# Two-layer block on one core: order and step numbers of the first layer's vector, scalar and store work

## The chip, the cores and the metric

The kernel runs on one core of a Trainium2 chip. The metric is device time in microseconds, the median of several runs. The engines are named as the profile names them: PE (TensorE, with PEld for its weight loads), DVE (VectorE), ACT (ScalarE), POOL (GpSimd) and SP (SyncE, which here only issues DMAs). Each works through its own instructions in the order in which the program lists them, and they meet at semaphores.

## What is computed

Two layers, each `x + attention(norm(x)) * silu(ffn(norm(x)))`, over 4 sequences of 512 tokens with 512 features. The change lies in the first layer and in the first work of the second.

```python
# layer 0: softmax attention, 32 query heads of 16 over 8 key/value heads, no mask
q, k, v = xn @ Wq, xn @ Wk, xn @ Wv
attn = softmax((q @ k.T) * 16 ** -0.5).astype(float16)
s = (attn @ v) @ Wo
# layer 0: FFN between Walsh-Hadamard transforms (fwht)
h = fwht(xn * SU_ug) / 64
h = silu(h @ W_gate.T * (Wscale_gate * 64)) * (h @ W_up.T * (Wscale_up * 64))
h = fwht(h * SU_dp) / 64
g = silu(h @ W_down.T * (Wscale_dp * 64))
x = x + s * g
# layer 1: gated delta-rule recurrence (6 heads of 64) and an FFN with sign(up), sign(down) weights
x = x + recurrent(layernorm(x)) * silu(ffn_sign(layernorm(x)))
```

## The kernel before

The kernel is one program in two parts, `layer0` and `layer1`. `layer1` is not touched, apart from what the end of `layer0` prepares for it.

**The loop.** Layer 0 runs a loop over steps `t` that every engine walks in its own block of code, `for t in range(TEND)`. `b = t // 64` is the batch (sequence) and `m = t % 64` the step in it; there are 256 steps of four batches and 39 steps behind them (`b == B`, called batch 4 here), in which the last batch is finished and layer 1 begun. A step number such as `OUT_STEP` or `K_STEP` says at which `m` a piece of work is listed. Step numbers stand in tuples at the top of the file (lines 37 to 57).

**Attention.** A score group is one block of 128 queries of one key/value head with its 4 query heads: four matmuls of 128x512 into four PSUM banks. It is listed at every odd step. PE's `scores` (L1134) waits until the four exponentials of the group before have read the banks (`p_ready`). DVE then takes four row maxima (`row_max`, L638), each followed by ACT's `exps` (L944), which writes the probabilities. The time from one group's scores to the next is called a pair below, because it spans two steps. `turn_probs` (L352) on SP transposes the probabilities by DMA at even steps, and PE's `weigh` (L1150) multiplies them with the values for two groups at a time, at every fourth step. DVE transposes tokens (L676, L700), and PE's projection by `wo` is L1122.

**What is laid around it.** In steps `m < 32` PE does the down projection of the batch before, 6 matmuls a step (L1179). In steps `m >= 32` it does the gate and up projections, 8 matmuls a step (L1165), gate chunks at even steps and up chunks at odd ones. A chunk goes through ACT `tanh_gate` (L956), DVE `gate_mul` (L644) and `up_mul` (L657), then ACT `high_rows` (L913, a 16-bit copy of the product in `th`) and POOL `low_rows` (L454, the remainder). `up_mul` writes the buffer that `low_rows` of the chunk before has read. In an odd step `m > 32` the order on DVE is row maximum 0, `gate_mul`, row maxima 1 to 3, `up_mul`. On ACT it is `tanh_gate`, exponential 0, `high_rows`, exponentials 1 to 3.

**Keys and queries.** `project_k` (L1102) is listed at `K_STEP` 57 on PE, and ACT's `evict_k` (L920) at 58. It copies the keys of the next batch to the buffer `kst`, and waits until all heads of the present batch have been loaded from `kst` and `qst` (DMAs of SP: `load_k` L310 at `m % 8 == 6`, `load_q` L320 at `m % 8 == 2`). The last of these, a `load_q`, is listed on SP at step 58.

**The end of a block of tokens.** For each of the four blocks of 128 tokens of the batch before: DVE `scale_down` (L711) at `DOWN_END` 8, 16, 24, 32; ACT `tanh_down` (L964) one step later; DVE `second_gate` (L716) one more step later, which is listed ahead of the row maxima of that step. At `OUT_STEP` the attention output is projected (PE L1122), at +1 comes `gated` (L722) on DVE and POOL's add (L459), at +3 the store of `x1` from the buffer `th` (SP L388). There are two `th` buffers, so `tanh_down` of block 2 waits for the store of block 0, and the first `up_mul` of the next batch, which uses the same memory, for the store of block 2.

**Batch 0** has extra work: the FFN weights are transformed and split into 16-bit halves. PE transforms (L1075, L1076) and transposes the normed rows of later batches (L1054); ACT `evict_x` (L876) copies these transposes out, at the steps `TURN_STEP`; POOL adds pairs of weights (L413, L414, L423, L424, L448).

**Batch 4** has 8 steps of attention left (`ATT = 8` is the distance between a step and the exponentials listed at it). At `m == 3` DVE lists the first work of layer 1: `next_stats` (L766, L769), `weight_max` (L727, twice) and `next_scale`, at 9 `next_split` (L783, L786), at 12 `weight_low` (L751), at 13 `column_scales`; ACT `weight_high` (L969) at 9. SP loads the raw weights at `RAW_AT` (L344), ACT takes their signs at `SIGN_AT` (L975). PE transposes the split rows at `NEXT_STEP` (L1200), ACT evicts them at `EVICT_STEP` (L979), and `project_next` (L1211) ends the layer.

## Time and profile before

| | us |
|---|---|
| median of 3 runs | 1400.39 (1399.33 to 1401.78) |
| the profiled execution | 1401.55 |
| its span (first to last instruction) | 1399.8 |
| PE busy | 1259.5 (90%) |
| DVE busy | 1050.2 (75%) |
| ACT busy | 787.6 (56%) |
| POOL busy | 524.7 (37%) |
| layer 0, up to the first layer-1 operation | 768.8 |

How it is read: busy time is the sum of the operations of an engine. In the timeline a row is one operation, or a run of equal ones ("x4"), with its start and length; the bracket is the time that the engine stood idle before it and what ended that idle time. "PEclk" is the clock that TensorE was granted in each slice, in tenths of full speed. Layer 1 takes the last 631 us, in four like stretches.

### The profile page before, as it was taken

Reading aid. Unit: us, or ns where it says so; the run is one execution under the profiler, and the core shown is the slowest. Engines: PE = TensorE matmul, PEld = TensorE weight load, DVE = VectorE, ACT = ScalarE, POOL = GpSimd, SP = SyncE. Lnnn points to the kernel's source line nnn. Section 1 sums busy time; section 2 is a strip of 40 time slices with the busy share of each in tenths; the row PEclk is TensorE's granted clock in tenths of the full one; section 3 lists DMA queues with packets and bytes.
Section 4 is the critical chain, followed back from the end, with each engine's and each line's share of the span. In section 5 each row is a group of like instructions: output and inputs, shape, how many; then the busy total and the mean of one; then the engine's idle time right before and its main releaser. Section 6 shows DMA issues by size and latency. Waiting matters only on the chain. (4 is left out here: it accounts for less than half of the span.)

```text
span 1399.8 us, 23475 instructions
## 1 busy us (share of the span) xinstructions
PE 1259.5 (90%) x8738; PEld 643.5 (46%) x8738; DVE 1050.2 (75%) x1823; ACT 787.6 (56%) x1306; POOL 524.7 (37%) x434
## 2 busy tenths in 40 slices
PE   5777977988798897889959999999999999999998
PEld 2332333333333333333324545865477555855475
DVE  6678875778677786778883986868956976968845
ACT  4775765667676685667836752355433652355431
POOL 3589852012211221012301573328431573328431
PEclk9999999999999999999989999999999999999999
DMA  6655643676567765786777024010131024001121
GB/s 238 199 138 95 110 84 72 108 155 136 104 112 156 141 118 96 137 158 119 127 208 283 22 58 90 10 38 27 44 81 38 9 58 91 17 31 40 42 40 46
DMA packets 346561, 135.59 MB, mean 97 GB/s; under 512 B 312176, under 2 KB 333392, under 8 KB 343888
## 3 DMA queue, kind: packets, MB, share of 16 engines
q1 hardware_dynamic: 334032, 132.52, 42.4%
q10 hardware_dynamic: 12416, 1.57, 1.0%
q8 instruction: 70, 1.15, 0.4%
q14 instruction: 43, 0.35, 0.1%
HBM read 44.87 MB, written 17.87 MB: 45 GB/s over the span
## 5 line engine op out<-in xcount | busy, mean ns | idle before, releaser
L1165 PE MATMUL bank<-rows,both 128*128 128x512 f16 x1024 | 250.2, 391 | 38.8 <-DVE th L657 22.4
L944 ACT ACTIVATE probs<-vpair,top_n 128x512 f16<-128x512 f32 x256 | 170.5, 687 | 141.3 <-DVE top_n L638 141.2
L638 DVE TENSOR_REDUCE top_n<-vpair 128x1 f32<-128x512 f32 x256 | 169.3, 682 | 64.5 <-PE bank L1134 64.0
L1179 PE MATMUL bank<-dn,h 128*128 128x512 f16 x768 | 182.6, 386 | 0.0
L1165 PEld LDWEIGHTS bank<-rows,both 128*128 128x128 f16 x1024 | 95.9, 100 | 176.5 <-DVE th L657 36.6
L944 ACT ACTIVATE probs<-bank,top_n 128x512 f16<-128x512 f32 x256 | 164.4, 687 | 0.0
L638 DVE TENSOR_REDUCE top_n<-bank 128x1 f32<-128x512 f32 x256 | 163.3, 678 | 0.0
L454 POOL TENSOR_TENSOR h<-th,h 128x512 f16<-128x512 f32 x61 | 70.5, 1155 | 225.0 <-ACT h L913 225.0
L2246 PE MATMUL bank<-rows,both 128*128 128x512 f16 x512 | 117.3, 380 | 0.0
L1179 PEld LDWEIGHTS bank<-dn,h 128*128 128x128 f16 x768 | 71.3, 99 | 93.7 <-issue 17.8
L2262 PE MATMUL bank<-both,hid 128*128 128x512 f16 x512 | 111.2, 379 | 0.0
L2230 PE MATMUL bank<-rows,both 128*128 128x512 f16 (+1 forms) x456 | 104.0, 379 | 0.9 <-PEq L160 0.9
L1134 PE MATMUL vpair<-qk 32*128 32x512 f16 x256 | 50.5, 390 | 35.4 <-ACT probs L944 35.4
L2262 PEld LDWEIGHTS bank<-both,hid 128*128 128x128 f16 x512 | 50.1, 98 | 60.4
L2246 PEld LDWEIGHTS bank<-rows,both 128*128 128x128 f16 x512 | 48.1, 99 | 55.0
L2230 PEld LDWEIGHTS bank<-rows,both 128*128 128x128 f16 (+1 forms) x456 | 43.6, 98 | 55.6 <-issue 4.4
L1621 POOL TENSOR_TENSOR big<-big,both 128x384 f32<-128x384 f32 x32 | 32.0, 1025 | 94.5 <-DMA big<-t_scratch 70.2
L657 DVE SCALAR_TENSOR_TENSOR th<-bank,hsc,tg 128x512 f32<-128x512 f32 x64 | 48.0, 751 | 22.1 <-POOL h L454 10.8
L467 POOL TENSOR_TENSOR otok<-oblk,rl 128x256 f16<-128x256 f32 x25 | 15.5, 619 | 125.0 <-DVE rl L684 125.0
L956 ACT ACTIVATE tg<-bank,usc 128x512 f32<-128x512 f32 x64 | 44.0, 687 | 32.5 <-DVE th L657 21.6
L1575 POOL TENSOR_TENSOR hid<-sil 128x512 f32<-128x512 f32 x24 | 33.1, 1379 | 62.4 <-DVE sil L1695 62.4
L1134 PEld LDWEIGHTS vpair<-qk 32*128 32x128 f16 x256 | 12.5, 91 | 91.8 <-ACT probs L944 54.3
(357 smaller groups left out, 2556.5 us busy)
## 6 DMA issues: line engine op xcount, KB each, us to landing
h<-in_ug SPq DMA_DIRECT2D x8, 1024.0 KB, 6.5
lt_scratch<-big SPq DMA_DIRECT2D x16, 384.0 KB, 2.8
dn<-in_down SPq DMA_DIRECT2D x2, 2048.0 KB, 11.5
x_scratch<-th SPq DMA_DIRECT2D x16, 256.0 KB, 3.1
res<-x_scratch SPq DMA_DIRECT2D x16, 256.0 KB, 4.3
out_x<-res SPq DMA_DIRECT2D x16, 256.0 KB, 2.0
both<-in_w SPq DMA_DIRECT2D x2, 1548.0 KB, 11.4
t_scratch<-tok SPq DMA_DIRECT2D x16, 192.0 KB, 2.1
```

Source lines behind the costliest of these rows:

```text
L454: pool.tensor_tensor(h16(ft, 1), row32, h16(ft, 0), ALU.subtract).then_inc(S["row_lo"], 1)
L638: v.tensor_reduce(top_n[:, i:i + 1], SC_[n % G][:, :], AX.X, ALU.max, negate=True).then_inc(S["max_done"], 1)
L657: v.scalar_tensor_tensor(row32, GB[n % 2][:, :], hsc[:, ft:ft + 1], tg[:, :], ALU.mult, ALU.mult).then_inc(S["gb_took"], 1)
L944: a.activation(probs[:, k % TAKEN, j * T:(j + 1) * T], SC_[j][:, :], ACT.Exp, bias=top_n[:, i:i + 1]).then_inc(S["p_ready"], 1)
L956: a.activation(tg[:, :], GB[n % 2][:, :], ACT.Tanh, scale=gsc[:, ft:ft + 1]).then_inc(S["tanh_ready"], 1)
L1134: pe.matmul(SC_[j][:, :], qs[32 * j:32 * j + 32, u % SLOTS, qt * P:(qt + 1) * P], ks[32 * j:32 * j + 32, u % SLOTS, :], start=True, stop=T ...
L1165: mm = pe.matmul(GB[n % 2][:, :], w[:, kt, col:col + P], xnb(b, kt), start=r == 0, stop=r == 2 * KT - 1)
L1179: mm = pe.matmul(bk, h16(ft, r // 2)[:, rows], dn16(ft, r % 2), start=j == 0 and r == 0, stop=j == FT - 1 and r == 2)
L1575: pool.tensor_tensor(sqf[m % 2], sil[:, ORDER[m], :], sil[:, ORDER[m], :], ALU.mult).then_inc(S["sq_r"], 1)
L2230: mm = pe.matmul(bk, lhs(i, kt), rhs(j, kt), start=n == 0, stop=n == 3 * KT - 1)
L2246: mm = pe.matmul(fbank[ht % 2][:, :], up[:, kt, ht * P:(ht + 1) * P], x_half(i, kt), start=kt == 0 and i == 0, stop=kt == KT - 1 and i == 1)
L2262: mm = pe.matmul(fbank[tt % 2][:, :], hid[:, i, ht, tt * P:(tt + 1) * P], down[:, ht, :], start=ht == 0 and i == 0, stop=ht == HT - 1 and ...
```

## The change

It moves work and adds or removes none, apart from one empty step at the end of the loop.

- `K_STEP` 57 becomes 61: `project_k` on PE and `evict_k` on ACT are listed four steps later.
- `OUT_STEP` and `OUT_LAST` (20, 22, 28, 35) become (20, 22, 26, 34): blocks 2 and 3 are projected, gated and stored earlier. `TEND` becomes 294.
- ACT: `tanh_down` becomes the first of its step instead of one of the last; `high_rows` stands ahead of exponential 0 instead of behind it; `evict_x` stands ahead of the exponentials instead of behind them.
- The first work of layer 1 is listed later: the DVE block from step 3 to step 8, `next_split` 9 to 11, `weight_low` 12 to 14, `column_scales` 13 to 15, ACT `weight_high` 9 to 11, the exponential of `negA` 10 to 12; the transposes and their evictions 19 and 20 to 21 and 22; the first three raw loads 11, 12, 13 to 13, 14, 15; two of the signs 22, 23 to 23, 24.

```diff
-OUT_STEP = (20, 22, 28, 35)
-OUT_LAST = (20, 22, 28, 35)
-NEXT_STEP, EVICT_STEP = 19, 20
+OUT_STEP = (20, 22, 26, 34)
+OUT_LAST = (20, 22, 26, 34)
+NEXT_STEP, EVICT_STEP = 21, 22
 XRES_STEP = (17, 19, 24, 25)
-Q_STEP, V_STEP, K_STEP = 5, 43, 57
+Q_STEP, V_STEP, K_STEP = 5, 43, 61
...
-RAW_AT = (11, 12, 13, 21, 23, 24, 25, 26)
-SIGN_AT = (18, 19, 20, 21, 22, 23, 26, 34)
+RAW_AT = (13, 14, 15, 21, 23, 24, 25, 26)
+SIGN_AT = (18, 19, 20, 21, 23, 24, 26, 34)
...
-                if b == B and m == 3:
+                if b == B and m == ATT:
                     next_stats()
                     weight_max(0)
                     next_scale()
...
-                if b == B and m == 9:
+                if b == B and m == ATT + 3:
                     next_split()
                     weight_scales()
-                if b == B and m == 12:
+                if b == B and m == ATT + 6:
                     for kt in range(KT):
                         weight_low(kt)
-                if b == B and m == 13:
+                if b == B and m == ATT + 7:
                     column_scales()
...
+                if b and m - 1 in DOWN_END:
+                    tanh_down((b - 1) * TT + DOWN_END.index(m - 1))
                 if b < B and m > FFN_STEP and m % 2:
                     tanh_gate(b, (m - FFN_STEP) // 2)
-                if paired:
-                    exps(G * (ta // 2))
                 if 0 <= fb < B and fm > FFN_STEP and t % 2:
                     high_rows(fb, (fm - FFN_STEP) // 2)
-                if paired:
-                    for j in range(1, G):
-                        exps(G * (ta // 2) + j)
                 if t in TURN_STEP:
                     evict_x(KT + TURN_STEP.index(t))
+                if paired:
+                    for j in range(G):
+                        exps(G * (ta // 2) + j)
...
-                if b and m - 1 in DOWN_END:
-                    tanh_down((b - 1) * TT + DOWN_END.index(m - 1))
-                if b == B and m == 9:
+                if b == B and m == ATT + 3:
                     weight_high()
-                if b == B and m == 10:
+                if b == B and m == ATT + 4:
```

## Rows read from the trace of the kernel before

**Rows 1.** Page, section 2: POOL busy and TensorE clock, 40 slices of 35 us

```profile
POOL 3589852012211221012301573328431573328431
PEclk9999999999999999999989999999999999999999
```

**Rows 2.** Waits: engine, line, releaser; total us, times, longest us

```profile
ACT kst L920 <- DMA qk<-qst: 19.8, 3, 7.5
DVE th L716 <- ACT th L964: 19.8, 11, 7.8
PE bank L1054 <- ACT rows L876: 13.1, 5, 3.6
DVE th L657 <- POOL h L454: 10.8, 47, 0.6
```

**Rows 3.** Timeline, 328 to 334 us, batch 1: start, length, engine, line, operation [idle]

```profile
328.75 0.39 PE L1134 MATMUL vpair<-qk 32*128 32x512 f16 x2
...
329.17 0.69 DVE L638 TENSOR_REDUCE top_n<-vpair 128x1 f32<-128x512 f32 x1 [0.41 <-PE bank L1134]
...
332.48 0.75 DVE L657 SCALAR_TENSOR_TENSOR th<-bank,hsc,tg 128x512 f32<-128x512 f32 x1 [0.23 <-POOL h L454]
...
333.61 0.39 PE L1134 MATMUL vpair<-qk 32*128 32x512 f16 x2
```

**Rows 4.** Timeline, 214 and 376 to 389 us, around evict_k, batches 0, 1

```profile
214.69 0.60 ACT L920 ACTIVATE kst<-bank 128x512 f16<-128x512 f32 x1 [5.61 <-DMA qk<-qst]
...
376.75 0.39 PE L1134 MATMUL vpair<-qk 32*128 32x512 f16 x2
...
379.57 2.44 SPq L320 DMA_DIRECT2D qk<-qst  x4
383.34 0.60 ACT L920 ACTIVATE kst<-bank 128x512 f16<-128x512 f32 x1 [7.45 <-DMA qk<-qst]
...
388.93 0.39 PE L1134 MATMUL vpair<-qk 32*128 32x512 f16 x2
```

**Rows 5.** Timeline, 264 to 300 us, around tanh_down, batch 1

```profile
264.06 0.39 PE L1134 MATMUL vpair<-qk 32*128 32x512 f16 x2 [0.24 <-ACT probs L944]
...
265.16 1.28 DVE L638 TENSOR_REDUCE top_n<-vpair 128x1 f32<-128x512 f32 x2
...
294.95 0.58 SPq L388 DMA_DIRECT2D x_scratch<-th  x1
...
295.48 1.29 ACT L944 ACTIVATE probs<-vpair,top_n 128x512 f16<-128x512 f32 x2 [1.28 <-DVE top_n L638]
...
298.01 0.39 PE L1134 MATMUL vpair<-qk 32*128 32x512 f16 x2 [0.24 <-ACT probs L944]
...
298.30 0.63 ACT L964 ACTIVATE th<-fd 128x512 f32<-128x512 f32 x1 [0.34 <-DMA x_scratch<-th]
...
299.57 1.28 DVE L638 TENSOR_REDUCE top_n<-vpair 128x1 f32<-128x512 f32 x2
```

**Rows 6.** Timeline, 313 to 318 us, steps 33 to 35 of batch 1

```profile
313.98 1.21 SPq L388 DMA_DIRECT2D x_scratch<-th  x1
...
317.38 0.75 DVE L657 SCALAR_TENSOR_TENSOR th<-bank,hsc,tg 128x512 f32<-128x512 f32 x1 [3.34 <-DMA x_scratch<-th]
```

**Rows 7.** Timeline, 60 to 62 us, batch 0: an evict_x and its waiter

```profile
60.62 0.59 ACT L876 ACTIVATE rows<-bank 128x512 f16<-128x512 f16 x1
...
61.26 0.38 PE L1065 MATMUL bank<-amax,allone 128*128 128x1 f32 x2 [2.06 <-ACT rows L876]
```

**Rows 8.** Timeline, 720 to 763 us, end of layer 0

```profile
720.70 0.61 PE L1134 MATMUL vpair<-qk 32*128 32x512 f16 x2 [13.20 <-ACT probs L944]
...
721.64 5.14 PE L1179 MATMUL bank<-dn,h 128*128 128x512 f16 x12
...
741.81 0.70 DVE L700 STREAM_TRANSPOSE oT<-otok 128x512 f16<-128x512 f16 x1
...
762.84 5.45 PE L1211 MATMUL bank<-rows,both 128*12 128x512 f16 x24
```

## The prediction, made before the changed kernel was run

> **What bounds the kernel now.** I read the page first, then the table of waits, then the timeline of each place that the diff touches. The page says that TensorE was granted nearly its full clock, but for one slice at 700 to 735 us [rows 1]. PE is 90% busy over the span, so what can be won is its idle time and its slow stretches in layer 0. Layer 1, 631 us, has no edit. Within layer 0 the pace is not set by PE alone: two groups share a cycle scores, row maxima, exponentials, next scores, and whatever is queued between these on DVE or ACT lengthens a pair. The waits table names the places that the diff aims at: `evict_k` behind a DMA, 19.8 us in 3 waits; `second_gate` behind `tanh_down`, 19.8 in 11; PE behind an `evict_x`, 13.1 in 5; `up_mul` behind POOL's `low_rows`, 10.8 in 47 [rows 2]. A wait in that table is idle time of an engine and not yet time of the kernel, so each is priced below from the spacing of the scores.
>
> **Keys at step 61.** In batch 1 the copy of the keys waits for the last `load_q`, issued at 379.57, and ACT stands 7.45 us with the exponentials queued behind it; the pair takes 388.93 - 376.75 = 12.18 us [rows 4]. An ordinary pair of the same shape takes 333.61 - 328.75 = 4.86 [rows 3]. The gain is 12.18 - 4.86 = 7.3. Is the wait gone or only moved? The next scores would now come at 376.75 + 4.86 = 381.6, and the copy at step 62 stands behind those of that pair, 4 us or so later, at about 385.7 on the clock of now; the load had landed by 383.3. Gone, by 2 us. Batch 2 is taken by the table: 19.8 in three waits, less 7.45 and less 5.61 of batch 0 [rows 2, 4], leaves 6.7, and I count 6.7. In batch 0 steps 57 to 63 also carry down-weight transposes through the same single bank (`DN_AT`), so the projection at 61 should lengthen that pair; between no gain and 5.6 I take 2.7. The moved projection itself (4 matmuls) leaves one PE-filled pair and fills another: nothing. Past `load_k` on SP at step 62, which waits for `evict_k`: `load_k` is for heads needed several pairs later, and SP is idle at that time in batch 1 (it issues nothing between the `load_q` and the copy that it waits for). I price it at nothing; if SP had no slack it would cost the load's 2.5 us. **Sum: 7.3 + 6.7 + 2.7 = 16.7.**
>
> **high_rows ahead of exponential 0.** In the gate/up stretch `up_mul` waits 0.23 for POOL's `low_rows`, which waits for `high_rows`, behind exponential 0 [rows 3]. The row maximum that exponential 0 needs starts at 329.17 and ends at 329.86 [rows 3], and ACT, which comes out of `tanh_gate` at about 329.55, has 0.3 us free there, so the 0.62 us copy delays exponential 0 by at most 0.3 and exponential 1 not at all. Low end: the wait alone, 10.8 us in 47 [rows 2], counted only in the pairs that PE or `up_mul` bounds, about 6 of 16 in a batch: 6 x 0.23 = 1.4. High end: the whole copy, 0.62, in those six, 3.7. I take 2.5 a batch, 2.9 in batch 3 (no projections that fill PE), 1.1 in batch 0, where POOL is full: **9.0**, range 3 to 13.
>
> **tanh_down ahead of the exponentials.** At a step such as 264.06 the row maximum comes 265.16 - 264.06 = 1.10 after the scores, against 329.17 - 328.75 = 0.42 where nothing stands in front [rows 5, 3]. `second_gate` is late because the tanh came behind four exponentials. Ahead of them it is done before: 0.68 gained at blocks 0 and 1. But moving it also makes ACT do it before the exponentials of its own step, and for block 2 it waits for the store of block 0: issued at 294.95, the tanh starts at 298.30 after a wait on that DMA, while the exponentials of the same step start at 295.48 now [rows 5]. **This is a new wait.** Behind it are queued the four exponentials, and behind these PE's next scores and DVE's next maxima. The tanh still starts at 298.30, exponential 0 at 298.93, and the next scores 298.01 - 295.48 = 2.53 later, at 301.46: 3.45 later than now. The pair behind has its row maximum at 0.42 and not at 299.57 - 298.01 = 1.56, which gives back 1.14. So from there the batch runs 2.3 us late against now, and the 1.36 of blocks 0 and 1 are swallowed by the wait, unless the store comes earlier. SP works back to back in this stretch, so I take it that it doesn't. **Cost 2.3 in each of batches 1, 2 and 3.** In batch 4 block 2 has no exponentials behind it (8 steps only): nothing.
>
> **OUT_STEP 28 to 26, 35 to 34.** The first `up_mul` of the next batch waits 3.34 us for the store of block 2, issued at 313.98 [rows 6], with row maxima queued behind it. Two steps earlier (a pair, 3.7 us) the store lands before `up_mul` comes: 3.34 gained in three batches, 10.0. The four `wo` matmuls are only moved within steps where PE waits. At the start of a batch `high_rows` between exponentials 0 and 1 leaves too (about 0.45, the last pair of the gate/up stretch) in batches 2 to 4: 1.3. **Together with the cost above: 10.0 + 1.3 - 6.9 = 4.4.**
>
> **evict_x in batch 0.** PE waits for transposed rows that ACT copies behind four exponentials, as at 61.26 after a copy at 60.62 [rows 7]; 13.1 in 5 waits [rows 2]. Ahead of the exponentials the copy comes some 2.5 us earlier, but the exponentials each 0.6 later. From below 1, from above most of the 13.1 less six copies of 0.6, or 9.5. But POOL bounds part of this stretch, eight and nine tenths busy in the slices from 70 to 140 us [rows 1], and where it does an earlier copy gives nothing. I take **5**.
>
> **The end of layer 0.** Now the block of layer 1 holds the row maxima and PE stands 13.20 us before the scores at 720.70 [rows 8]. I looked for what it would leave if moved: the same DVE work still stands before `next_split` and `weight_low`, and the tokens' last transpose (741.81) and so the last output projections wait for it; `project_next` starts at 762.84 behind them [rows 8]. By the new order the transposed tokens come at about 742 again. PE gains 13 us early and waits them out later. I take **0**, from 6 worse to 2 better on this path, and the case that the bubble is really gained is a rival.
>
> Beside this a rule of the Trainium skill, in sentences the sum does without. Rows first: after the 13.20 us idle, 12 down matmuls took 5.14 us, 0.43 each, and 24 matmuls at 762.84 took 5.45, 0.227 each [rows 8]: the half clock of 1.2 GHz against 2.4. "TensorE: Matmul & The Clock Gate", section "HAM oscillation — how this bites in real kernels", says that a burst after an idle stretch starts cold and that the penalty is half of the throttled time; the trace agrees. It speaks against this change in one respect: the new hold at step 25 makes a fresh idle of PE of some 4 us per batch, which by it could add about 1 to 3 us each; it speaks for it at `evict_k`, where the idle goes.
>
> **Sum.** 16.7 + 9.0 + 4.4 + 5 + 0 = 35.1. From the profiled execution, 1401.55 - 35.1 = 1366.4; the median lies 1.16 below it, so 1365.3. I say **1365**.
>
> **The rivals.**
> 1. *The gains are smaller.* `high_rows` and `evict_x` pay at their low ends (3 and 1), and the hold at step 25 costs 4 in each batch rather than 2.3, as clock is lost with it: 16.7 + 3 + (11.3 - 12) + 1 - 2 at the end = 18, time 1382. For it: six of the terms are a choice between far ends. Chance 0.22.
> 2. *The end of the layer is won.* If what fixed the end was PE's work and not DVE's chain, the 13.20 us come free: 1352. For it: the largest single idle of PE. Against it: DVE's work is the same and ends at the same time. Chance 0.12.
> 3. *The key wait stays.* The change would not do what it says if the copy at step 62 still waited: for `load_q` of the next steps, or if SP is so late that its landing follows. Then 16.7 goes: 1382. Against it: the load had landed at 383.3. Chance 0.05.
> 4. *Slower.* The hold at step 25 feeds itself: with the copy of keys gone, SP's queue loses its pause of some 7 us per batch and comes later to the stores, each later store holding the exponentials one for one. It decides from about 12 us of extra lateness in each of three batches: 1365 + 36 = 1401 and beyond, say 1404. Against it: SP has idle time between batches. Chance 0.04.
>
> **How the numbers follow.** The forecast has 0.57, with its own range 1357 to 1374. The range 1352 to 1384 takes in rivals 1, 2 and 3 and leaves out their tails and rival 4. A difference of 0.2% (2.8 us) is about what a measurement of this kernel can tell from none. Faster: all cases but rival 4 and a thin edge, 0.93; same 0.03; slower 0.04.
>
> **What would show it.** Right: no `kst <- DMA` wait, the pair at steps 59 to 61 near 4.9; a wait `ACT L964 <- DMA x_scratch` of about 3 us in front of the exponentials of step 25, batches 1 to 3; no wait of `up_mul` on `x_scratch`; `second_gate` without a wait at steps 10 and 18; the first operation of layer 1 at 768.8 less 35, with PE idle behind step 8 of batch 4 instead of at step 5. Wrong: layer 1 longer or shorter than 631, a wait of SP on `evict_k` that reaches the scores, or a layer-0 tail that starts 13 us sooner behind the same batch 4.

## The result and the profile after

The changed kernel takes 1367.84 us (median of 4 runs, 1366.1 to 1369.64) against 1401.09 for the kernel before beside it: 0.9758 of its time, 95% interval 0.9728 to 0.9787. The forecast was 1365, from 1352 to 1384. The profiled execution has a span of 1367.5 us, 32.3 less than before; the sum had said 35.1. The first matmul of layer 1 starts at 738.34 (769.17 before), so 30.8 of the 32.3 lie in layer 0; the other 1.4 are in layer 1 (629.2 us long, 630.6 before), which no edit touches.

The page first: instruction counts and busy times are those of before within 6 us, so the whole difference is idle time and clock.

```profile
PE 1256.4 (92%) x8738; PEld 644.2 (47%) x8738; DVE 1045.0 (76%) x1823; ACT 785.3 (57%) x1306; POOL 525.1 (38%) x434
```

The waits that answer [rows 2] (total us, times, longest us):

```profile
DVE th L716 <- ACT th L964: 16.9, 6, 6.3
ACT th L964 <- DMA x_scratch<-th: 16.3, 3, 5.9
...
ACT probs L944 <- DMA probsT<-probs: 10.7, 1, 10.7
...
PE bank L1052 <- ACT rows L876: 5.8, 4, 2.8
...
DVE th L657 <- POOL h L454: 1.7, 1, 1.7
```

No wait of `evict_k` on a DMA is left (19.8 us before), nor the wait of the first `up_mul` on the store. `low_rows` holds `up_mul` once and not 47 times; PE's wait behind `evict_x` has fallen from 13.1 to 5.8, and `second_gate` no longer waits at steps 10 and 18. And there is a wait of 16.3 us, `tanh_down` of block 2 on the store of block 0, three times, longest 5.9. In the kernel before, the same table has it so:

```profile
ACT th L964 <- DMA x_scratch<-th: 1.4, 3, 0.8
```

Lines after 1030 are two lower than before (L1132 is `scores`, L1052 the transpose of rows, L1163 the gate/up matmul).

Around the keys, batch 1 (timeline: start, length, engine, line, operation; compare [rows 4]):

```profile
366.92 0.39 PE L1132 MATMUL vpair<-qk 32*128 32x512 f16 x2
...
370.24 2.44 SPq L320 DMA_DIRECT2D qk<-qst  x4
...
371.45 0.39 PE L1132 MATMUL vpair<-qk 32*128 32x512 f16 x2
...
375.58 0.59 ACT L920 ACTIVATE kst<-bank 128x512 f16<-128x512 f32 x1
```

The pair that took 12.18 takes 371.45 - 366.92 = 4.53, and the copy at 375.58 waits for nothing.

Around step 25, batch 1 (compare [rows 5]):

```profile
286.67 0.39 PE L1132 MATMUL vpair<-qk 32*128 32x512 f16 x2 [0.47 <-ACT probs L944]
...
287.66 1.50 SPq L388 DMA_DIRECT2D x_scratch<-th  x1
...
291.30 0.63 ACT L964 ACTIVATE th<-fd 128x512 f32<-128x512 f32 x1 [4.77 <-DMA x_scratch<-th]
...
291.83 1.25 ACT L944 ACTIVATE probs<-vpair,top_n 128x512 f16<-128x512 f32 x2
...
294.29 0.61 PE L1132 MATMUL vpair<-qk 32*128 32x512 f16 x2 [3.33 <-ACT probs L944]
...
294.84 4.36 PE L1177 MATMUL bank<-dn,h 128*128 128x512 f16 x13
...
299.13 0.39 PE L1132 MATMUL vpair<-qk 32*128 32x512 f16 x2
```

This is the new wait: the exponentials stand behind the tanh and the tanh behind a store. The pair takes 294.29 - 286.67 = 7.62 us where 3.67 is its length without a hold. The 13 matmuls behind it took 4.36 us, 0.335 each against 0.227 at full clock [rows 8], and PE has no gap from 294.29 to the next scores at 299.13: this next pair, 4.84 us, is as long as PE's slow matmuls make it.

The end of layer 0 (compare [rows 8]):

```profile
687.45 1.26 ACT L944 ACTIVATE probs<-vpair,top_n 128x512 f16<-128x512 f32 x2 [10.69 <-DMA probsT<-probs]
...
689.95 1.05 PE L1148 MATMUL bank<-probsT,vaug 128*32 128x256 f16 x16 [9.82 <-issue]
690.93 6.66 PE L1177 MATMUL bank<-dn,h 128*128 128x512 f16 x24
...
710.01 0.70 DVE L700 STREAM_TRANSPOSE oT<-otok 128x512 f16<-128x512 f16 x1
...
710.86 1.86 PE L1120 MATMUL bank<-wo,oT 128*128 128x512 f16 x4 [2.46 <-DVE oT L700]
...
732.02 5.45 PE L1209 MATMUL bank<-rows,both 128*12 128x512 f16 x24
```

PE's 13.20 us before the scores of step 7 are gone. In their place stand 9.82 before `weigh` and 2.46 before the first projection, with slow matmuls behind both. The last transpose is still what it waits for.

What ends the first of the two is on SP. The exponentials at 687.45 waited 10.69 us for a transpose of the probabilities, and SP issued it at 681.06, behind 15 loads for layer 1 that stand there from 667.51 on:

```profile
667.51 1.16 SPq L326 DMA_DIRECT2D rows<-x_scratch  x1
...
680.53 0.43 SPq L334 DMA_DIRECT2D both<-in_out_scale  x1
681.06 11.74 SPq L352 DMA_TRANSPOSE probsT<-probs  x4
```

The kernel before had the same loads at the same place; there the wait of the same exponentials is put down to the row maxima:

```profile
711.26 0.43 SPq L334 DMA_DIRECT2D both<-in_out_scale  x1
711.80 14.57 SPq L352 DMA_TRANSPOSE probsT<-probs  x4
...
718.17 1.28 ACT L944 ACTIVATE probs<-vpair,top_n 128x512 f16<-128x512 f32 x2 [14.14 <-DVE top_n L638]
```

Counted from the scores of step 5, that transpose landed after 14.0 us before and after 14.2 us now, and these exponentials started after 14.1 and 14.3. Two waits ended there within 0.2 us, one on DVE and one on SP's loads. The change moved the one that showed.

For the whole of layer 0, pair lengths worked out from the starts of the scores:

| pair | before | after |
|---|---|---|
| steps 59 to 61, batches 1, 2 | 12.18, 11.80 | 4.54, 4.54 |
| 25 to 27, batches 1, 2, 3 | 3.67, 3.67, 3.67 | 7.62, 8.48, 8.75 |
| 27 to 29, batches 1, 2, 3 | 4.81, 4.70, 5.29 | 4.84, 4.78, 4.62 |
| 33 to 37 (two pairs), batches 1, 2, 3 | 13.14, 13.20, 13.21 | 9.62, 9.62, 9.62 |
| the pairs from 39, 47, 51, 55 (and 43 in batch 3), batches 1 to 3 | 4.85 to 5.50 | 4.54 |
| step 5 of batch 4 to the first layer-1 matmul | 65.1 | 65.2 |

### The profile page after: what moved, and what is told of

Read it like the earlier page. It is cut to its first block and busy times, and to the rows that moved or that the text cites. A ratio compares the mean times of both kernels' runs of the same rounds, so it can differ in the third digit from the quotient of the medians.

```text
span 1367.5 us, 23475 instructions
## 1 busy us (share of the span) xinstructions
PE 1256.4 (92%) x8738; PEld 644.2 (47%) x8738; DVE 1045.0 (76%) x1823; ACT 785.3 (57%) x1306; POOL 525.1 (38%) x434
## 2 busy tenths in 40 slices
DMA packets 346561, 135.59 MB, mean 99 GB/s; under 512 B 312176, under 2 KB 333392, under 8 KB 343888
## 5 line engine op out<-in xcount | busy, mean ns | idle before, releaser
L1163 PE MATMUL bank<-rows,both 128*128 128x512 f16 x1024 | 244.9, 385 | 13.5 <-DVE th L657 9.7
L1163 PEld LDWEIGHTS bank<-rows,both 128*128 128x128 f16 x1024 | 95.6, 99 | 148.1 <-issue 21.6
L2244 PE MATMUL bank<-rows,both 128*128 128x512 f16 x512 | 118.8, 383 | 0.0
L1132 PE MATMUL vpair<-qk 32*128 32x512 f16 x256 | 50.8, 392 | 26.6 <-ACT probs L944 26.5
L459 POOL TENSOR_TENSOR th<-fd,xres 128x512 f32<-128x512 f32 x16 | 18.5, 1156 | 96.6 <-DVE fd L722 96.6
L1633 POOL TENSOR_TENSOR os_<-os_,both 128x6 f32<-128x6 f32 x16 | 23.3, 1459 | 80.6 <-DVE os_ L1991 80.6
L1686 DVE SCALAR_TENSOR_TENSOR rows<-pre,both,rows 128x512 f32<-128x512 f32 x36 | 40.8, 1133 | 17.1 <-ACT rows L2067 16.2
## 6 DMA issues: line engine op xcount, KB each, us to landing
both<-in_w SPq DMA_DIRECT2D x2, 1548.0 KB, 11.3
```

The costliest lines, as they stand in the source:

```text
L1132: pe.matmul(SC_[j][:, :], qs[32 * j:32 * j + 32, u % SLOTS, qt * P:(qt + 1) * P], ks[32 * j:32 * j + 32, u % SLOTS, :], start=True, stop=T ...
L1163: mm = pe.matmul(GB[n % 2][:, :], w[:, kt, col:col + P], xnb(b, kt), start=r == 0, stop=r == 2 * KT - 1)
L1686: v.scalar_tensor_tensor(c[:, :], src[:, i:i + T], cw[:, cm, i:i + 1], c[:, :], ALU.mult, ALU.add).then_inc(S["conv"], 1)
L2244: mm = pe.matmul(fbank[ht % 2][:, :], up[:, kt, ht * P:(ht + 1) * P], x_half(i, kt), start=kt == 0 and i == 0, stop=kt == KT - 1 and i == 1)
```

## The experiments

Each was timed beside the kernel before; the ratio is to that. The medians of the kernel before were 1400.0 (experiments 1 to 4), 1400.1 (5 to 7 and 10), 1403.1 (8, 9, 11) and 1403.0 us (12), and 1401.1 for the changed kernel above. "More" and "less than the changed kernel" are differences of medians from these different sessions. By the ratios the same differences are 19.6 us for experiment 1, 7.0 for 2, 13.7 for 3, 8.0 for 4, 6.7 for 6 and 7.4 for 7, each good to some 5 us; the intervals of 2, 4, 6 and 7 only just clear that of the changed kernel. Lengths of pairs are from one profiled execution each.

**1. The keys back at step 57.**

```diff
-Q_STEP, V_STEP, K_STEP = 5, 43, 61
+Q_STEP, V_STEP, K_STEP = 5, 43, 57
```

> The changed kernel with K_STEP put back to 57, nothing else. My sum: the wait of evict_k on the last load_q comes back in batches 1 and 2, pairs of 12.2 and 11.8 us in place of 4.5, less 0.8 for the projection that moves back: +7.3 and +6.9; in batch 0 a stall of some 5.5 again but without the pairs of 7.5 and 10.1 behind it, +2.7. Theory (the key wait was the largest term): about 1367.8 + 16.5 = 1384, range 1381 to 1387. Rival (the pairs around step 59 are set by PE or by high_rows, and the wait would only be taken over): below 1373.

Measured 1386.12 us, ratio 0.9898 (0.9881 to 0.9914): 18.3 more than the changed kernel. The wait is back as it was:

```profile
ACT kst L920 <- DMA qk<-qst: 19.7, 3, 7.3
```

The pairs at 59 took 12.2 and 11.9 us in batches 1 and 2, and in batch 0 the three pairs from 57 to 63 took 28.3 us against 25.5 in the changed kernel: 2.8. The key wait is the largest term, and nothing took it over.

**2. evict_x behind the exponentials again.**

```diff
-                if t in TURN_STEP:
-                    evict_x(KT + TURN_STEP.index(t))
                 if paired:
                     for j in range(G):
                         exps(G * (ta // 2) + j)
+                if t in TURN_STEP:
+                    evict_x(KT + TURN_STEP.index(t))
```

> The changed kernel with evict_x behind the exponentials again. It is only in batch 0 that anything can differ. The changed kernel reaches step 33 of batch 0 5.95 us sooner than the kernel before. Theory (this comes from evict_x, the only edit of that stretch but for tanh and high_rows, which have nothing to do there): +5 to +7, about 1373.5, and the scores of step 33 back near 135.4 us. Rival (POOL's weight pairs bound the stretch, so that the early lead of 9 us at step 21 is not evict_x's to keep): +0 to +2.

Measured 1373.92 us, ratio 0.9808 (0.9790 to 0.9827): 6.1 more. The scores of step 33 of batch 0 came at 136.2 us (129.5 in the changed kernel). At step 21 the changed kernel led this one by 11.3 us and at step 33 by 6.7. Of both, 1.5 stood already at the very first scores (48.1 and 49.6 us; in kernels with the changed kernel's start these came at 46.7 to 49.2), which leaves 9.8 and 5.2. So 4.6 of it was lost between steps 21 and 33, where POOL adds its weight pairs, but not the rest.

```profile
PE bank L1052 <- ACT rows L876: 13.2, 6, 3.6
```

**3. high_rows between exponentials 0 and 1 again.**

```diff
-                if 0 <= fb < B and fm > FFN_STEP and t % 2:
-                    high_rows(fb, (fm - FFN_STEP) // 2)
...
+                if paired:
+                    exps(G * (ta // 2))
+                if 0 <= fb < B and fm > FFN_STEP and t % 2:
+                    high_rows(fb, (fm - FFN_STEP) // 2)
                 if paired:
-                    for j in range(G):
+                    for j in range(1, G):
                         exps(G * (ta // 2) + j)
```

> The changed kernel with high_rows between exponentials 0 and 1 again. Theory: the pairs that the changed kernel has at 4.54 us go back to 4.85 (five or six per batch), the first two pairs of a batch from 4.37 and 3.67 to 4.65 and 4.13: 6 x 0.31 + 0.7 = 2.6 in each of batches 1 to 3, about 1 in batch 0 and 0.7 in batch 4: +9, about 1377, range 1374 to 1379. Rival (PE bounds these pairs, the gain came from other edits): +0 to +3, and no change of the 4.54 pairs.

Measured 1378.72 us, ratio 0.9856 (0.9839 to 0.9873): 10.9 more. The pairs of 4.54 us went back to 4.86 and 5.14, and:

```profile
DVE th L657 <- POOL h L454: 12.5, 48, 1.7
```

Ending a wait of 0.23 us in each pair, far down in the table, was worth some 9 to 11 us of the kernel.

**4. tanh_down of block 2 behind the exponentials, the others first.**

```diff
-                if b and m - 1 in DOWN_END:
+                if b and m - 1 in DOWN_END and m - 1 != DOWN_END[2]:
                     tanh_down((b - 1) * TT + DOWN_END.index(m - 1))
...
+                if b and m - 1 == DOWN_END[2]:
+                    tanh_down((b - 1) * TT + 2)
```

> The changed kernel, but tanh_down of block 2 alone goes back behind the exponentials; those of blocks 0, 1 and 3 stay first. In the changed kernel the pair of step 25 takes 7.62, 8.48 and 8.75 us in batches 1, 2 and 3 where 3.67 is its length without a hold, and the pair behind it 4.84, 4.78 and 4.62. Theory (the hold on the store of block 0 costs wall time one for one): the three pairs fall to 3.67 and the pairs behind them stay at 4.7 to 5.3: 4.0 + 4.8 + 5.1 = 13.9 less, at most 1.5 of it lost to row maxima behind a late second_gate, so about 1355, range 1353 to 1358. Rival (the hold is bubble that the next store or the first up_mul of the batch takes back, since the store of block 2 is listed only some pairs later): gain under 4, 1364 or above, with a wait of up_mul on the store.

Measured 1356.93 us, ratio 0.9701 (0.9680 to 0.9723): 10.9 less than the changed kernel, 3 us short of the arithmetic of the pairs and inside the range. The wait on the store has fallen from 16.3 to:

```profile
ACT th L964 <- DMA x_scratch<-th: 2.3, 3, 1.4
```

The pair at 25 took 4.22, not 3.67, in each batch. By the ratio the gain is 8.0 and not 10.9; the profiled execution of the changed kernel has dearer holds than most (see below). The edit also moves the tanh of block 2 in batch 4, and there it cost 1.4 (66.6 us from the scores of step 5 to layer 1, for 65.2). So the hold that the prediction named is real and is the change's largest loss.

**5. The kernel before with tanh_down first in its step, and nothing else of the change.**

```diff
+                if b and m - 1 in DOWN_END:
+                    tanh_down((b - 1) * TT + DOWN_END.index(m - 1))
                 if b < B and m > FFN_STEP and m % 2:
                     tanh_gate(b, (m - FFN_STEP) // 2)
...
-                if b and m - 1 in DOWN_END:
-                    tanh_down((b - 1) * TT + DOWN_END.index(m - 1))
```

> The kernel before with one edit of the change: tanh_down first in its step, in all blocks. Theory, as in the prediction: the exponentials of step 25 are held for the store of block 0, 3.45 us of which 1.14 comes back in the pair behind, in batches 1 to 3: +7, and nothing behind it takes that back; about 1407, range 1404 to 1411. Rival: the kernel before has a second wait on a store 20 us later, the 3.3 us of the first up_mul, and a batch that comes later by 2 to 3 us waits there as much less, so that the edit alone costs 0 to 2: 1400 to 1402, with the pair at step 35 falling from 8.7 to about 6.

Measured 1408.38 us against 1400.08, ratio 1.0051 (1.0032 to 1.0069): half a per cent slower, as the theory had it. But half of the mechanism is the rival's. In the profiled execution the pairs at 25 took 8.1, 8.3 and 6.7 us, the pairs behind them grew from 4.8, 4.7, 5.3 to 5.7, 7.0, 5.8 (13 matmuls took 0.40 to 0.50 us each there), and the pairs at 35 fell from 8.7, 8.9, 8.9 to 5.6, 6.1, 6.1. The wait of `up_mul` on the store went from 8.8 us to:

```profile
DVE th L657 <- DMA x_scratch<-th: 1.2, 2, 0.6
```

A batch that comes later waits less at the next store. From the start of a batch to step 37 the edit cost 1.1, 3.2 and -0.2 us in batches 1, 2 and 3 of the profiled execution, about 4 in all, where the prediction's arithmetic has 7. The end of the layer, where the edit also acts, became 1.5 shorter (63.6 us for 65.1). That execution (1404.26) was the fastest of seven; why the median lies 4 us above it, these traces don't tell.

**6. OUT_STEP back at 28 and 35.**

```diff
-OUT_STEP = (20, 22, 26, 34)
-OUT_LAST = (20, 22, 26, 34)
+OUT_STEP = (20, 22, 28, 35)
+OUT_LAST = (20, 22, 28, 35)
```

> The changed kernel with OUT_STEP and OUT_LAST (20, 22, 28, 35) again. Theory (the store of block 2 two steps sooner is what frees the first up_mul): the two pairs from step 33 to 37 go from 9.6 back to 13.1 us in batches 1 to 3: +10.5, about 1378, range 1376 to 1380. Rival (the later batch of the changed kernel, held at step 25, would have found the store landed anyway): +0 to +4, below 1372.

Measured 1373.38 us, ratio 0.9806 (0.9789 to 0.9822): 5.5 more, half of what was expected. The two pairs from 33 to 37 took 11.5, 10.4 and 10.6 us, not 13.1. The pair at 27, to which the projection returns, grew to 5.8, 6.5 and 5.7 with the slow matmuls in it. The end of the layer was 1.6 us shorter than the changed kernel's (63.6 from the scores of step 5). Here too the batch reaches the first `up_mul` late, held at step 25 already, and finds the store nearly landed:

```profile
DVE th L657 <- DMA x_scratch<-th: 3.1, 2, 2.0
```

Experiments 5 and 6 say the same thing from two sides: the two stores' holds lie one behind the other on one queue, and each hides part of the other.

**7. Block 0 projected at step 19, its store issued at 21 ahead of load_k.**

```diff
-OUT_STEP = (20, 22, 26, 34)
+OUT_STEP = (19, 22, 26, 34)
...
+                if b >= 0 and any(m == o + (2 if o == 19 else 3) for o in out_step(b + 1)):
...
+                    sp.dma_start(x1_dram[b, tt], x1[:, tt % 2, :]).then_inc(S[f"x1_out{tt % 2}"] if n < NT - 2 else W["x1_last"], 16)
                 if ta % STEPS == 6 and 1 < ta // STEPS + 2 < NU:
                     load_k(ta // STEPS + 2)
```

> The changed kernel with block 0 projected at step 19 in place of 20 and its store issued at step 21, ahead of load_k, where the changed kernel issues it at 23 behind load_k; batch 4 keeps its steps. tanh_down stays first. Theory (the hold at step 25 is the landing of this store, and nothing else): the store lands 2.7 us or more sooner, the pair at step 25 falls from 7.6 to 8.8 to 4.2 or 5, and the pair at steps 21 to 23, 6.69 us with project_q behind gated, to about 4: 3 x (4 + 2.7) = 20 less, about 1348, range 1345 to 1356. Rival (the load of heads that the store is moved ahead of, or the DMA engines themselves, then set the pace): the two pairs shorten, but scores of a later unit wait for their heads, 1360 or more.

Measured 1359.94 us, ratio 0.9705 (0.9683 to 0.9726): 7.9 less than the changed kernel, where 20 had been expected; the profiled execution (1356.09) is the fastest of its four and lies 13.3 below the changed kernel's. The hold at step 25 is gone (4.23, 4.22, 4.22 us, and 3.69, 3.68, 3.68 behind it), and the pair at 21 fell from 6.69 to 5.14, not to 4. But the pair at 33 grew from 5.08 to 7.20, 7.28 and 6.76:

```profile
303.59 1.27 ACT L944 ACTIVATE probs<-vpair,top_n 128x512 f16<-128x512 f32 x2 [1.48 <-DMA probsT<-probs]
303.60 0.62 PE L1148 MATMUL bank<-probsT,vaug 128*32 128x256 f16 x16 [2.05 <-DMA probsT<-probs]
```

Now exponentials and `weigh` wait for the transposes of the probabilities, which SP issues. SP has the same work as before and is asked for it sooner; that it has fallen behind is the reading that the next experiment tests. These 6 us over three batches are part of what is missing from the 20. The rest lies between the median and the profiled execution, and no trace shows it.

**8. The loads of xres and the stores of x1 issued by POOL, block 0 at step 19.**

```diff
-                    sp.dma_start(xres[:, tt % 2, :], d["x"][b, tt * P:(tt + 1) * P, :]).then_inc(S[f"xres_in{tt % 2}"], 16)
...
-                    sp.dma_start(x1_dram[b, tt], x1[:, tt % 2, :]).then_inc(S[f"x1_out{tt % 2}"] if n < NT - 2 else W["x1_last"], 16)
...
+                    pool.dma_start(xres[:, tt % 2, :], d["x"][b - 1, tt * P:(tt + 1) * P, :]).then_inc(S[f"xres_in{tt % 2}"], 16)
...
                     residual(n)
+                    pool.wait_ge(S["x1_ready"], n + 1)
+                    pool.dma_start(x1_dram[b - 1, tt], x1[:, tt % 2, :]).then_inc(S[f"x1_out{tt % 2}"] if n < NT - 2 else W["x1_last"], 16)
```

The loads are issued at `XRES_STEP` as before, the stores one step sooner, at the output step + 2.

> The changed kernel with the loads of xres and the stores of x1 issued by POOL and not by SP, each store right behind POOL's add, and block 0 projected at step 19. tanh_down stays first. Theory (SP's queue, back to back in the first half of a batch, sets the stores' landing and, once these are sooner, the transposes of the probabilities): no hold at step 25, pairs at 25 and 27 near 4.2 and 3.7, and the pairs from 33 to 37, 7.2 and 4.5 in the run with the store moved within SP's queue, back to 5.1 and 4.5: 2 us less in each of three batches than that run, 1353, range 1348 to 1357. Rival (the DMA engines, not the issuing queue, are what is full, or POOL's issue is dear enough to hold its adds and low_rows): 1359 or more, with exponentials that wait for the transposes as before.

Measured 1352.29 us, ratio 0.9641 (0.9616 to 0.9666), against 0.9705 for the run before this one. The pairs at 33 are 5.08, 5.09 and 5.24 again, and of the waits for transposes, 16.6 us in five in that run, 12.2 are left, 10.8 of them the one at the end of the layer:

```profile
ACT probs L943 <- DMA probsT<-probs: 12.2, 2, 10.8
```

(L943 is `exps` in this kernel.) POOL pays 0.55 us for most issues and has the time. The transfers are the same 135.59 MB, so what was full was SP's issuing queue and not the DMA engines.

**9. The first work of layer 1 where it was** (step 3 and the other numbers of the kernel before).

```diff
-                if b == B and m == ATT:
+                if b == B and m == 3:
                     next_stats()
```

> The changed kernel with the first work of layer 1 where it was: the DVE block at step 3 of batch 4, next_split 9, weight_low 12, column_scales 13, weight_high 9, transposes 19, raw loads and signs as in the kernel before. Theory, as in the prediction (the move shifts 13 us of PE idle from step 5 to step 8 and DVE's chain ends at the same time): from the scores of step 5 to the first layer-1 operation 65 us as in both kernels, 1367.8 within 2, PE idle 13 us before the scores of step 7. Rival (the move did gain and another edit of the end, the projection at 34 or tanh first, lost it again): 1371 or more.

Measured 1368.13 us, ratio 0.9743 (0.9720 to 0.9767), the changed kernel's time. The idle stretch moved back to the scores of step 7, and from step 5 to layer 1 it took 64.4 us against 65.2:

```profile
690.95 0.60 PE L1132 MATMUL vpair<-qk 32*128 32x512 f16 x2 [13.43 <-ACT probs L944]
```

The transpose of the probabilities behind SP's loads landed 13.9 us after the scores of step 5, as in the other two kernels.

**10. weight_low and column_scales at step 18.**

```diff
-                if b == B and m == ATT + 6:
+                if b == B and m == ATT + 10:
                     for kt in range(KT):
                         weight_low(kt)
-                if b == B and m == ATT + 7:
+                if b == B and m == ATT + 10:
                     column_scales()
```

> The changed kernel with weight_low and column_scales of the last stretch at step 18 of batch 4 in place of 14 and 15, so that the last tokens' reciprocal, scale_down and the last transpose (L684, L711, L700) stand ahead of 7 us of DVE work. Theory (the end of layer 0 is set by DVE's chain up to that transpose, behind which stand the last output projections): PE no longer idles 2.5 us at 708.4 and has no slow matmuls behind it: 4 less, about 1364, range 1362 to 1366. Rival (ACT's chain of signs and evictions, or PE's own work, sets the end): no change within 1 us, the idle time turns up in front of turn_next or project_next.

Measured 1371.98 us, ratio 0.9796 (0.9776 to 0.9817): no gain, 4 more than the changed kernel; in the profiled execution the end of the layer took 1.9 more and the batches before it 1.3 less. The last transpose did come sooner (701.19 us, where it had been at 710.01), and PE did not wait for it. Then:

```profile
711.64 1.91 ACT L975 ACTIVATE both<-probs 128x2048 f16<-128x2048 f32 x1 [7.79 <-DVE both L751]
...
727.89 0.61 ACT L964 ACTIVATE th<-fd 128x512 f32<-128x512 f32 x1
...
730.01 1.88 PE L1120 MATMUL bank<-wo,oT 128*128 128x512 f16 x4 [2.62 <-DVE fd L722]
```

The signs wait for `weight_low`, a tanh stands behind them, and PE's last but one projection behind the tanh.

**11. The same with two signs behind that tanh.**

```diff
-RAW_AT = (13, 14, 15, 21, 23, 24, 25, 26)
-SIGN_AT = (18, 19, 20, 21, 23, 24, 26, 34)
+RAW_AT = (13, 14, 15, 21, 23, 24, 25, 29)
+SIGN_AT = (18, 19, 20, 21, 27, 28, 30, 34)
```

> weight_low and column_scales at step 18 as in the earlier run, and two signs that stood ahead of tanh_down of block 2 of batch 4 moved behind it: SIGN_AT 23, 24 to 27, 28, 26 to 30, and the last raw load from 26 to 29. Theory (the earlier move gained 4 us at the first output projection and lost 6 behind signs that hold the tanh, which held the last but one projection for 2.6 us and cost clock): the end of layer 0 comes 4 to 5 us sooner than in the changed kernel, 1363, range 1361 to 1366. Rival (PE's own work and the slow clock behind its idle stretch set the end): 1367 or more.

Measured 1365.99 us, ratio 0.9734 (0.9713 to 0.9754), which the intervals don't tell from the changed kernel's 0.9758. PE's own last work is sooner, but the next wait stands ready:

```profile
726.09 5.45 PE L1209 MATMUL bank<-rows,both 128*12 128x512 f16 x24
...
730.80 1.15 POOL L459 TENSOR_TENSOR th<-fd,xres 128x512 f32<-128x512 f32 x1 [5.21 <-DVE fd L722]
...
733.95 2.46 PE L2228 MATMUL bank<-rows,both 128*128 128x512 f16 x8 [2.40 <-PEq L160]
```

PE ends at 731.5 and enters layer 1 at 733.95, after POOL's last add. Counted from the scores of step 5 of batch 4, the projection began 2.5 us sooner than in the changed kernel, 1.0 of it was left at the entry, and layer 1 took 1.2 longer (630.4 us). The kernel before has 630.6 and, with only `tanh_down` moved (experiment 5), 629.0, so this much comes and goes without an edit.

**12. Experiments 8, 10 and 11 together, no sign between the last two tanh.**

```diff
-SIGN_AT = (18, 19, 20, 21, 23, 24, 26, 34)
+SIGN_AT = (18, 19, 20, 21, 27, 28, 34, 35)
```

> The run with POOL's queue and block 0 at step 19, together with weight_low and column_scales at step 18 and the signs 4 to 7 at 27, 28, 34, 35 (last raw load at 29), so that no sign stands between the third and the fourth tanh_down of batch 4. In the run with two signs moved, PE's last projection ended 5.5 us sooner than in the changed kernel, but PE then waited 2.4 us at the entry of layer 1, 0.87 in the others, with POOL's last add late behind the last tanh. Theory (that last tanh, held by the sign at step 30, is what the entry waits for): the end of layer 0 comes 3 to 4 us sooner than with POOL's queue alone, ratio to the kernel before 0.962, 1349 where the kernel before takes 1402, range 1346 to 1352. Rival (whatever is left of the signs runs into layer 1 and is paid there, or the entry waits for the store): no gain, 1352 or more, with layer 1 longer than 629.

Measured 1351.36 us, ratio 0.9629 (0.9608 to 0.9650): with experiment 8 the fastest here, and not to be told from it. (The 5.5 us of the expectation compared times of two executions; 2.5 is the part that the end of the layer has.) The time lies in the theory's range, the trace is the rival's:

```profile
720.16 1.91 ACT L974 ACTIVATE both<-probsT 128x2048 f16<-128x2048 f32 x1 [2.06 <-DMA probsT<-in_downw]
...
722.68 1.67 PE L2227 MATMUL bank<-rows,both 128*128 128x512 f16 x7 [1.75 <-PEq L160]
```

PE was done at 720.9; ACT's last sign, held by a load of raw weights, ended at 722.07, and layer 1 began behind it. The end took 65.2 us from step 5, as in the changed kernel and 1.1 more than in experiment 8. The four executions with the changed kernel's own end (experiments 1, 2, 3 and 7) took 65.3 each. Every rearrangement of this end tried here moved the wait by an engine and left the length within 2 us. None moved SP's 15 loads for layer 1, which stand ahead of the last transposes of the probabilities in all of them. What the end would take without that is open.

## Why the prediction was right, and where its terms were off

By place, from the starts of the scores in the two profiled executions:

| us gained | counted | measured |
|---|---|---|
| batch 0 | 8.8 | 6.6 |
| batch 1 | 10.8 | 10.7 |
| batch 2 | 10.7 | 9.6 |
| batch 3 | 4.4 | 3.9 |
| batch 4 to step 5 | 0.4 | 0.5 |
| end of layer 0 | 0 | -0.1 |
| layer 1 | 0 | 1.4 |
| before the first scores | 0 | -0.3 |
| sum | 35.1 | 32.3 |

Layer 0 alone fell short of the sum by 4.3 us. The 1.4 of layer 1 came from no term and are luck.

*Keys: 16.7.* Right in size and place. The undo cost 18.3 in the medians; by the pairs 7.7 and 7.3 in batches 1 and 2, and 2.8 in batch 0, for which 2.7 had been taken between 0 and 5.6. That SP's slack covers the later `load_k` held.

*high_rows: 9.0.* Right. The undo cost 10.9 in the medians and, from the first scores to step 5 of batch 4, 8.9 in the profiled execution. The step of it that carried the value, a choice between the wait alone (1.4 a batch) and the whole copy (3.7), came out near the middle, at 2.5 in batches 1 and 2 by the pairs of experiment 3; batch 3 gave 3.7 and batch 0 only 0.6.

*evict_x: 5.* Right. 6.1 in the undo, 5.2 by step 33 when both are counted from their first scores.

*The end: 0.* The number is right (65.1 and 65.2 us), the account is not whole, and luck has a part in it. The prediction had PE gain 13 us early and wait them out later at DVE's last transpose. PE's idle stretch became only 3.4 us shorter, and it ended 16.6 us after the scores of step 5 before and 16.8 now, since the transposes of the probabilities behind SP's loads came no sooner. The prediction did not look at SP there. And the 0 is a sum of parts that cancel, one of which the prediction put at nothing (`tanh_down` in batch 4) and one of which it did not price (`OUT_LAST`):

| from the scores of step 5 to layer 1 | us |
|---|---|
| kernel before | 65.1 |
| with `tanh_down` first (experiment 5) | 63.6 |
| and the first work of layer 1 later (experiment 6) | 63.6 |
| and `OUT_LAST` at 26 and 34 (changed kernel) | 65.2 |
| the same, with the first work of layer 1 where it was (experiment 9) | 64.4 |

So moving layer 1's first work gave nothing or lost 0.8, `tanh_down` first gave 1.5 there and the earlier `OUT_LAST` took 1.6. These are single executions; those with one and the same end agree within 0.2 us. Experiments 9 to 12 show that the chain through DVE, then ACT's signs, then POOL's last add or ACT's last sign follow one another so closely that removing one gave at most 1 us at the entry of layer 1. The rival at 1352 (the bubble really won) did not come; with SP's loads where they stand PE could not have had those 13 us early.

*tanh_down and OUT_STEP together: 4.4.* The sign is right, and this is the mis-sized term. From the start of a batch to step 37 the changed kernel gained 0.9, 0.1 and 0.5 us in batches 1, 2 and 3, 1.5 in all, where 1.0 or 1.5 had been counted in each. Three steps in it:
- The place, the cause and nearly the price of the new wait at step 25 are right. The pair grew by 4.0, 4.8 and 5.1 us, which takes back what the tanh gained at blocks 0 and 1 (0.67 and 0.25, where 0.68 was counted for each); left is a batch later by 3.0, 3.9 and 4.2 us, where 3.45 was counted. The store of batch 1 was issued at 287.66, only 7.3 us sooner than before [rows 5], where the batch came 7.7 sooner, and landed at 291.2, after 3.6 us where it had taken 3.3. Other executions were cheaper: over the 21 such holds of the changed kernel and experiments 1, 2, 3, 9, 10 and 11 the pair took 6.8 to 8.8 us, 7.55 in the mean.
- "The pair behind gives back 1.14" failed in two of three batches. The row maximum was sooner, but the pair stayed at 4.84 and 4.78 (before 4.81 and 4.70), since 13 down matmuls took 4.36 us behind the 3.33 us that PE had stood. Only batch 3 gave back 0.7. This step is the mis-sized term: the hold with its pair behind cost 3.1, 4.0 and 3.5 us, and 2.3 was counted. Here the rule quoted in the prediction, that a burst after an idle stretch starts cold (the Trainium skill, "TensorE: Matmul & The Clock Gate", section "HAM oscillation — how this bites in real kernels"), decided a term that the sum had left to the row maxima. 13 x (0.335 - 0.227) = 1.4 us is what it took. The prediction had put 1 to 3 us a batch beside its sum and not into it. The traces agree with the rule in 15 of the 21 holds. In the other six the clock stayed full and the pair behind took 3.69 or 3.68, which is the 1.14 given back, as here in experiment 2, batch 1:

```profile
304.71 0.39 PE L1132 MATMUL vpair<-qk 32*128 32x512 f16 x2 [2.90 <-ACT probs L944]
...
305.04 2.98 PE L1177 MATMUL bank<-dn,h 128*128 128x512 f16 x13
...
308.39 0.39 PE L1132 MATMUL vpair<-qk 32*128 32x512 f16 x2 [0.38 <-ACT probs L944]
```

- "3.34 gained at up_mul" is right by the pairs (3.52, 3.58, 3.59 for steps 33 to 37) but the two holds were added as if each stood alone. Experiments 5 and 6 show that they are not additive: with the hold at 25 in place, `OUT_STEP` alone is worth 5.5 us and not 10; without `OUT_STEP`, the hold at 25 is half paid for by a shorter wait at 35.

*The fourth rival* (SP's queue falls behind) did not come in the changed kernel, but experiment 7 brought it up with one more gain on the same stretch: 2 us in each batch at step 33. The condition had been stated for stores; it was the transposes that were late.

*Batch 0* gave 6.3 us by its end, 6.6 from its first scores (8.8 counted). At step 33 the lead was 5.95 and at step 57 it was 3.34; the changed kernel had a pair of 6.38 for 5.00 at step 43, in which `up_mul` waited for POOL between two weight pairs (the 1.7 us that is left of that wait), and one of 10.73 for 9.18 at step 53. The second is no effect of the change: experiment 5, whose batch 0 is the kernel before's, has 10.46 there. The first stood in every kernel with `evict_x` first; experiment 2, without it, had 5.86 for 4.28 in the pair before instead. Its cause is open.

## What to carry to other kernels

Putting a short instruction ahead of others on an in-order engine is worth it only if its own last wait is over by then; look up what each copy of it waits for, since one in four here waited for a store and cost more than the two before it gave. Two waits on the same queue are one budget: price them together, by the time at which the queue serves the second. A row "waited for X" names the wait that ended last; another may end 0.2 us behind it, so look at every engine and at the issuing queue before counting an idle stretch as free. And at a seam between two stages read what is late next on every engine before you move the wait that shows: here four engines' last waits lay within some 3 us of one another.

## What the runs showed of the hardware

The granted clock could fall after short idle times of PE, and did not always: after 3.33 us without a matmul 13 matmuls took 0.335 us each, after 9.82 us 24 took 0.28 each, after 13.20 us 12 took 0.43 each; 0.227 is the time at full clock [rows 8]. In the 21 holds at step 25 the clock fell to half in 15, after idle times of 2.59 to 4.46 us, and stayed full in six, after 2.54 to 3.18, with 13 matmuls at 0.229 each. What tells the two apart between 2.6 and 3.2 us is open. A store of 256 KB landed 3.3 us after its issue in the kernel before (294.95) and 3.6 in the changed one (287.66), while SP issued back to back; the medians of all 16 are 3.1 and 2.8. Issued by POOL, such a store occupied POOL for 0.56 us, and landed 2.9 us (median) after its issue. Taking these eight DMAs a batch off SP (four loads, four stores), with the stores one step sooner, gave 0.6% of the kernel against the run with the store moved within SP. Fifteen loads in a row kept SP for 13.5 us (667.51 to 680.96) and held the transpose behind them.
